# A mixture-of-experts kernel on one core: the matrix engine's routed loop holds eight tiles in place of two, loads one set number a tile, and the expert columns move to another PSUM bank

## The reference

```python
scores = jax.nn.sigmoid(x @ gate_w)
...
_, selected_experts = jax.lax.top_k(masked_scores, K)
weights = jnp.take_along_axis(original_scores, selected_experts, axis=-1)
weights = weights / jnp.sum(weights, axis=-1, keepdims=True)
...
g = jax.lax.ragged_dot(xs, w_gate, group_sizes)
u = jax.lax.ragged_dot(xs, w_up, group_sizes)
d = jax.lax.ragged_dot(jax.nn.silu(g) * u, w_down, group_sizes)
out = d[unsort_idx].reshape(T, K, H)
expert_out = jnp.sum(out * weights[..., None], axis=1)
shared = jax.nn.silu(x @ sw_gate) * (x @ sw_up) @ sw_down
return (expert_out + shared).reshape(B, S, H)
```

## Time and profile before

| | |
|---|---|
| median of 3 runs | 2270.92 us (2268.97 to 2274.73) |
| the profiled execution | 2273.54 us, of which its span is 2271.7 us |
| PE busy | 1927.4 us, 85% of the span, 10056 matmuls |
| POOL busy | 1004.5 us, 44% |
| DVE and ACT busy | 1251.2 us (55%) and 581.7 us (26%) |

### The profile page before, as it was taken

The page is one execution under the profiler, slowest core; times in us unless marked ns, Lnnn a source line. Parts: engine busy times, 40 slices in busy tenths (PEclk is TensorE's granted clock), DMA queues, the critical chain, the costliest instruction groups (busy, mean ns, idle before and its releaser), DMA issues.

```text
span 2271.7 us, 34535 instructions
## 1 busy us (share of the span) xinstructions
PE 1927.4 (85%) x10056; PEld 1388.2 (61%) x10057; DVE 1251.2 (55%) x2357; ACT 581.7 (26%) x1291; POOL 1004.5 (44%) x552
## 2 busy tenths in 40 slices
PE   5956887877887489998799999999999999998991
PEld 3423443653333133333389988888888888887881
DVE  2555443556776757775674435555555555554550
ACT  3320222501114244453222212222222222221220
POOL 0000000002547355655025555556555757757886
PEclk9987998898996789999899999999999999999996
DMA  3033100503124457621124445556555656656999
GB/s 117 0 103 116 46 28 19 185 2 104 74 93 147 147 195 243 206 95 33 33 91 176 181 154 164 156 154 190 161 156 154 192 158 191 183 155 159 208 205 212
DMA packets 272642, 306.03 MB, mean 135 GB/s; under 512 B 40857, under 2 KB 184217, under 8 KB 272569
## 3 DMA queue, kind: packets, MB, share of 16 engines
q1 hardware_dynamic: 144216, 187.78, 25.7%
q10 hardware_dynamic: 106848, 66.34, 10.7%
q0 software_dynamic: 21504, 50.93, 9.5%
HBM read 186.42 MB, written 118.55 MB: 134 GB/s over the span
## 4 chain that ended last, share of the span: by engine, by line
PE 37%; POOL 7%; issue 3%; DMA 2%; DVE 1%; POOLq 0%; ACT 0%; DVEq 0%
PE psum L2515 15%; PE psum L2535 8%; PE psum L2520 7%; POOL X L2166 6%; PE psum L2540 4%; PE psum L2509 2%; DMA X<-d_y,f_slots 2%; PE psum L2502 1%; POOL e_gu_low L2131 0%; POOL e_d_low L2115 0%; DVE e_gu_low L2350 0%; POOL e_gu_high L2126 0%; POOL e_d_low L2116 0%; DVE e_d_low L2350 0%; DVE f_arena L2377 0%
## 5 line engine op out<-in xcount | busy, mean ns | idle before, releaser
L2515 PE MATMUL psum<-e_gu_high,e_rowT_high 128*128 (+1 forms) x1272 | 432.1, 341 | 52.2 <-issue 40.6
L2515 PE MATMUL psum<-e_gu_low,e_rowT_high 128*128 (+1 forms) x1272 | 410.7, 325 | 0.0
L2515 PEld LDWEIGHTS psum<-e_gu_high,e_rowT_high 128*128 128x128 f32 x1272 | 241.6, 190 | 87.4 <-issue 83.9
L2520 PE MATMUL psum<-e_gu_high,e_rowT_low 128*128 (+1 forms) x1272 | 257.6, 325 | 0.0
L2515 PEld LDWEIGHTS psum<-e_gu_low,e_rowT_high 128*128 128x128 f32 x1272 | 242.4, 191 | 3.7
L2216 ACT CAST e_rowT_high<-psum 128x512 fp32r<-128x512 f32 x127 | 74.5, 587 | 643.4 <-DVE psum L2297 602.3
L2520 PEld LDWEIGHTS psum<-e_gu_high,e_rowT_low 128*128 128x128 f32 x1272 | 214.8, 190 | 0.0
L2336 DVE COPY f_arena<-psum 128x512 f32<-128x512 f32 x127 | 87.9, 692 | 191.7 <-PE psum L2540 187.2
L2535 PE MATMUL psum<-e_d_high,e_midT_high 128*128 (+3 forms) x477 | 188.4, 395 | 1.0 <-ACT e_midT_high L2222 1.0
L2535 PE MATMUL psum<-e_d_low,e_midT_high 128*128 (+3 forms) x477 | 187.6, 393 | 0.0
L2124 POOL CAST e_gu_high<-f_gu_in 128x1408 fp32r<-128x1408 f32 x31 | 42.1, 1358 | 281.4 <-PE psum L2520 258.3
(11 more groups left out here) (382 smaller groups left out, 3856.7 us busy)
## 6 DMA issues: line engine op xcount, KB each, us to landing
d_sorted<-f_hs SPq DMA_DIRECT2D x32, 1048.0 KB, 10.2
d_y<-f_arena ACTq DMA_DIRECT2D x127, 256.0 KB
f_hs<-d_sorted ACTq DMA_DIRECT2D x492, 64.0 KB
f_gu_in<-in_L_ffn_w_gate SPq DMA_DIRECT2D x32, 704.0 KB
f_gu_in<-in_L_ffn_w_up SPq DMA_DIRECT2D x32, 704.0 KB
f_d_in<-in_L_ffn_w_down SPq DMA_DIRECT2D x32, 512.0 KB
d_y<-f_hs SPq DMA_DIRECT2D x8, 1024.0 KB, 5.7
f_d_in<-in_L_ffn_w_down SPq DMA_DIRECT2D x32, 192.0 KB
```

What stands on the lines that cost most here:

```text
L2515: nc.tensor.matmul(bank[:, 0:M].unsqueeze(1), rowT_high[par][:, k, :], w[:, bass.ds(buffer, 1), k, at:at + M], start=(k == 0 and n == 0), ...
L2520: last = nc.tensor.matmul(bank[:, 0:M].unsqueeze(1), rowT_low[par][:, k, :], gu_high[:, bass.ds(buffer, 1), k, at:at + M], start=False, st ...
```

## The change

Three edits, all in `routed_ffn`:

1. PE's loop holds eight tiles. Tiles 32 to 39 stand straight ahead of it, the loop makes 14 passes (tiles 40 to 151), and tiles 152 to 158 stand straight behind it.
2. The set number of a tile is read once and kept in a register: the one of the next tile is read between the up product and the down product of the present one, and the present one becomes the old one. Only at the top of a pass are two numbers read.
3. The asked expert columns go to the bank of the up product instead of the gate product's. PE has no wait on `weight_taken` any more, and ACT none either ahead of `copy_asked`; on DVE `take_weight` moves ahead of `low_blocks`, so that PE's wait on the low half covers it.

```diff
-        ASKED = [G[n][:, M:M + TOPK] for n in range(2)]
+        ASKED = [U[n][:, M:M + TOPK] for n in range(2)]
...
-        LOOP_END = (TILES - 3) // 2
+        PE_LOOP = 8
+        LOOP_END = (TILES - 1) // PE_LOOP
...
-            def copy_asked(i, par, place, loads, taken=None):
+            def copy_asked(par, place, loads):
 
                 act.wait_ge(row_loaded[place], LANDED * loads)
-                if taken is not None:
-                    act.wait_ge(weight_taken, taken)
                 nc.scalar.copy(ASKED[par], side[place][:, TOPK:2 * TOPK]).then_inc(asked_copied, 1)
...
                     turn_blocks(i + 1, (place + 1) % ROWS, fills)
+                    take_weight(i + 1, 1 - par, (place + 1) % ROWS)
                     low_blocks(i + 1, 1 - par)
-                    take_weight(i + 1, 1 - par, (place + 1) % ROWS)
...
-            def tile(i, par, e, old, turns=False, used=None, before=None, also=None, weighed=None):
-
-                if weighed is not None:
-                    pe.wait_ge(weight_taken, weighed)
+            def tile(i, par, e, old, turns=False, used=None, before=None, also=None, ahead=None):
+
...
+                following = set_of(ahead) if ahead is not None else None
                 if old is not None:
                     down(i - 1, 1 - par, old, before)
+                return following
...
-            with pe.Fori(SHARED_TILES // 2 + 1, LOOP_END) as n:
-                tile(n * 2, 0, set_of(n * 2), set_of(n * 2 - 1), used=n * 2 - 1, before=n * 2 - 2,
-                     weighed=n * 2 - SHARED_TILES + 1)
...
+            def routed_tiles(first, many, old):
+
+                e = set_of(first)
+                for q in range(many):
+                    following = tile(first + q, q % 2, e, old, used=first + (q - 1), before=first + (q - 2),
+                                     ahead=(first + (q + 1) if q + 1 < many else None))
+                    e, old = following, e
+
+            routed_tiles(SHARED_TILES, PE_LOOP, 1)
+            with pe.Fori(SHARED_TILES // PE_LOOP + 1, LOOP_END) as n:
+                routed_tiles(n * PE_LOOP, PE_LOOP, set_of(n * PE_LOOP - 1))
+            routed_tiles(LOOP_END * PE_LOOP, TILES - LOOP_END * PE_LOOP, set_of(LOOP_END * PE_LOOP - 1))
```

More of the change, by code:

```diff
@@ L2238, in routed_steps @@
                     copy_blocks(i + 1, 1 - par)
-                    copy_asked(i + 1, 1 - par, (place + 1) % ROWS, fills, i - SHARED_TILES if stores else None)
+                    copy_asked(1 - par, (place + 1) % ROWS, fills)
                 silus(i, par)
@@ L2271, in _ @@
             copy_blocks(SHARED_TILES, 0)
-            copy_asked(SHARED_TILES, 0, 0, 1)
+            copy_asked(0, 0, 1)
             for i in range(SHARED_TILES, SHARED_TILES + ROWS):
@@ L2462, in _ @@
             turn_blocks(SHARED_TILES, 0, 1)
+            take_weight(SHARED_TILES, 0, 0)
             low_blocks(SHARED_TILES, 0)
-            take_weight(SHARED_TILES, 0, 0)
             routed_steps(SHARED_TILES, 0, 1)
@@ L2584, in _ @@
                 shared_tile(i, also=table_ready)
-            tile(SHARED_TILES, 0, set_of(SHARED_TILES), 1, used=SHARED_TILES - 1, before=SHARED_TILES - 2, weighed=1)
-            tile(SHARED_TILES + 1, 1, set_of(SHARED_TILES + 1), set_of(SHARED_TILES), used=SHARED_TILES, before=SHARED_TILES - 1,
-                 weighed=2)
-            with pe.Fori(SHARED_TILES // 2 + 1, LOOP_END) as n:
-                tile(n * 2, 0, set_of(n * 2), set_of(n * 2 - 1), used=n * 2 - 1, before=n * 2 - 2,
-                     weighed=n * 2 - SHARED_TILES + 1)
-                tile(n * 2 + 1, 1, set_of(n * 2 + 1), set_of(n * 2), used=n * 2, before=n * 2 - 1,
-                     weighed=n * 2 + 2 - SHARED_TILES)
-            for i in range(LOOP_END * 2, TILES):
-                tile(i, i % 2, set_of(i), set_of(i - 1), used=i - 1, before=i - 2, weighed=i - SHARED_TILES + 1)
+            def routed_tiles(first, many, old):
[8 more added lines that the diff above has]
+            routed_tiles(LOOP_END * PE_LOOP, TILES - LOOP_END * PE_LOOP, set_of(LOOP_END * PE_LOOP - 1))
             turn_mid(TILES - 1, (TILES - 1) % 2)
```

## The result

The changed kernel takes 2234.15 us (median of 4 runs, 2232.09 to 2235.97) against 2271.49 us for the kernel before beside it (4 runs, 2268.97 to 2274.73): ratio 0.9835, 95% interval [0.9818, 0.9852]. That is 37.3 us less, where 32.4 us were forecast. The profiled execution took 2233.2 us, its span 2231.4 us.

What follows compares the result with a forecast made beforehand. PE was taken as the bound, its sequencer late once a pass. Gains of 31.2 (loop), 0.4 (entry) and 0.8 us (first routed tile) sum to 32.4, from the median 2270.92 to 2238.5 us; range 2231 to 2261.

Steps and rivals of the forecast that it cites:

- What bounds the kernel: Routed tiles: PE is the bound, and runs dry once a pass because its sequencer has nothing ready, 0.83 us a pass.
- The price of a top: Top of each pass: keeps branch and both loads, loses one wait step, 0.75 us each, 12 tops; 31.2 us gained.
- Taking the loads away gains nothing within a pass: Behind the down product: the two loads there were already hidden, 0.70 us from tile to tile, so removing them gains nothing.
- The entry: Entry to the loop's first pass: its cost of 0.4 us is gone from there.
- the first routed tile: First routed tile: PE, which waited 3.63 us for the pick, starts 0.8 us earlier.
- The load ahead of the down product costs nothing: Between up and down product: the 0.30 us load falls into a sequencer hole of 2.0 us; uncovered, up to 29 us.
- The other bank costs nothing: ACT's copy into the up bank: no conflict shown, nothing taken; bound 22 us.
- A tile takes 6.26 us within a pass: Routed loop: a tile without the stall of a top takes 6.26 us, used for 98 tiles, 613.5 us.
- Only what PE saves before the first gather counts: PE savings before the down product at 2020.44 move the whole tail forward; savings after it are worth nothing.
- the tail stays at 248.7: From first gather to end of span: POOL sets the pace, 248.7 us, forecast still about 249 us.
- near 1990.6: Sign in the changed kernel's trace: the first gather comes near 1990.6 us.
- The rival of the code fetched anew: At each loop branch the first code packet is fetched again: 2250 to 2270 us, 2260 in the middle; chance 0.16.

Runs made afterwards that it cites:

- oneload_only: The kernel before with one set load per tile ahead of the down product, still two tiles a pass, old bank and wait: 2253.53 us, ratio 0.9935.
- bank_only: The kernel before with only the third edit (expert columns to the up bank, pick moved ahead, its waits dropped): 2262.63 us, ratio 0.9975.
- loop2: The changed kernel with two tiles in a pass in place of eight: 2248.86 us, ratio 0.9910 to the kernel before.
- loop8_only: The kernel before with eight tiles in a pass alone, keeping two set loads per tile, old bank and wait: 2249.83 us, ratio 0.9914.
- twice_ahead: The changed kernel with every load ahead of the down product made twice: 2233.86 us, ratio 0.9843 to the kernel before.
- carried8: The changed kernel with no set load at the top of a pass, register moves carrying both sets over the branch: 2232.56 us, ratio 0.9835.

## Why the prediction was right

**What bounds the kernel.** Right. PE was held up by its own sequencer once a pass; no other engine came in its place. The waits for issue fell to 11 in the stretch where 45 stood.

**The price of a top, 0.84 - 0.09 = 0.75 us: too high.** This term of the sum was mis-sized. In the prediction's own terms, with a tile of 6.26 us, a top of the changed kernel costs 0.42 us (0.29 against a tile of straight code). The step that failed is the one by which a top keeps the branch and both loads "and loses one step of some 0.1 us". I had looked at the steps behind the branch alone. The runs show 0.27 us more that goes ahead of it, where seven steps in place of nine stand between the wait for the middle's high half and the branch (oneload_only); the dropped wait is 0.08 (bank_only). From the 0.82 of the kernel before these leave 0.47; loop2, which has both edits, measures 0.45. With 0.42 in place of 0.75 the loop gives 40.2 - 12 x 0.42 = 35.2 us, not 31.2.

**Taking the loads away gains nothing within a pass.** Right for the loop of two, where the tile behind a top takes 6.37 us with them and 6.36 without. What the prediction did not see is that the loop of eight needs this edit: loop8_only, with the loads behind the down product, has 74 waits, and the long loop alone gained 18.8 us where the prediction's sum gives it 30.6. The forecast held because the three edits came together.

**The entry, 0.4, and the first routed tile, 0.8 us.** Right: 0.9 measured at the first tile. 35.2 + 0.4 + 0.9 = 36.5, and the trace has 36.4.

**The load ahead of the down product costs nothing.** Right, shown by twice_ahead: even two are hidden.

**The other bank costs nothing.** Right: bank_only is 6.0 us faster, and 48 x 0.08 + 0.8 = 4.6 account for most of that.

**A tile takes 6.26 us within a pass.** Nearly right: one tile was read, and tiles differ by 0.09 us. The mean in straight code is 6.28, in carried8 6.30. The same 6.26 stood on both sides of the sum, so it changed the gain little: with 6.277 and 0.29 the loop gives 653.65 - 98 x 6.277 - 12 x 0.29 = 35.0 us.

**Only what PE saves before the first gather counts; the tail stays at 248.7.** Right within 0.7 us below and 3.1 above. The first gather came at 1981.0 and not near 1990.6: 5.6 of the 9.6 us are the difference of the two executions ahead of the stage, 4 the cheaper tops.

**The rival of the code fetched anew** did not come true with 8 tiles, and would have with 16. By the Trainium skill ("Runtime: NRT & Kernel Launch", Instruction fetch mechanics) a taken branch out of a window of two pages of 16 KiB causes a fetch, and PE has a memory of 128 KiB for code. The window doesn't agree with the traces: 3.1 packets, more than two pages, were kept. Nor is 128 KiB the longest body that is kept: 6.1 packets (100 KB) were not. What size the memory has no run shows. With the three packets that the fetch seems to run ahead, a body of eight tiles needs about 6 packets and one of 16 tiles about 9, so a memory of 8 would fit both (an estimate from the packet counts). My price for the fetch, 1 to 2.6 us a branch, was far too low: it is 6.6 to 7.1 us. Of the 12 tops 11 lie behind a branch, so the rival would have ended at 2238.5 + 11 x (6.6 - 0.75) = 2303 us, slower than before, and not at 2260. The decision for the forecast rested on a limit that no row of the trace before could give; that the pass of eight lay within it was luck.

**What stays open.** Where between 50 and 100 KB the limit lies; why tiles that nothing holds up take 6.24 to 6.33 us in turn; why the down product's waits come in another order with one load a tile; why the granted clock falls behind some holes and not behind others of the same length.

## What to carry to other kernels

When an engine waits for "issue" once a loop pass, don't charge the whole stall to the branch: count everything that its sequencer does from the last semaphore that it really waits for to the next tile's first matmul, on both sides of the branch, and move register loads and other waits ahead of that one, where they are free. Two steps there cost 0.27 us here. A lengthened loop can need such an edit even where the short one hid the loads. Make the body longer until the tops stop mattering, and no longer; here 8 tiles (50 KB of code) gave nearly all that straight code gives, and 16 tiles (100 KB) lost it all. Look at the code packets in a steady pass: none means that the body is kept.

## What the runs showed of the hardware that I had not expected

- A loop body of 3.1 code packets is kept and one of 6.1 is fetched anew in each pass, though straight code of 127 tiles has no wait for its code up to the first gather. The branch then takes 3.5 to 5.7 us, against 0.21, and some three packets more than the body are fetched.
- A hole of 1.6 us can be followed by some 3 us at a granted clock of 0.50 (the 1.2 GHz level), and another of the same length by none. Behind the branches of 3.5 to 5.7 us it was some 3 to 7 us at 0.50 each time, and the whole cost of such a branch was 6.6 to 7.1 us.
- A register load from SBUF takes the sequencer 0.64 us with its register steps (0.30 the load itself); two more at an exposed place cost 1.5 us of stall.
